# One line of 68 steps through a mixture's four blocks, and copies and splits of the causal heads on VectorE

## The reference

```
shared_out = silu(x @ shared_gate_w.T) * (x @ shared_up_w.T) @ shared_down_w.T
...
gate, up = jnp.split(gu, 2, axis=-1)
hmid = jax.nn.silu(gate) * up
y = jnp.einsum('tei,ehi->teh', hmid, down_proj)
out = jnp.einsum('teh,te->th', y, combine) + shared_out
```

```
score = jnp.einsum('bhqd,bhkd->bhqk', Q, K) / scale
score = score - 10000000000.0 * (1.0 - causal)
weights = jax.nn.softmax(score, axis=-1)
attn = jnp.einsum('bhqk,bhkd->bhqd', weights, V)
```

## Time and profile before

| | us |
|---|---|
| median of three runs | 1954.59 (1953.37 to 1954.68) |
| the profiled execution | 1949.53 |
| its span | 1947.7 |
| PE busy in the span | 1705.0 (88%) |
| VectorE busy | 1409.2 (72%) |
| ScalarE busy | 1158.7 (59%) |
| GpSimd busy | 311.4 (16%) |

### The profile page before, as it was taken

One profiled execution on the slowest core, in us unless ns is written; L12 is line 12 of the kernel. 1 busy time (PEld: TensorE's weight loads), 2 busy tenths in 40 slices (PEclk: granted clock), 3 DMA queues, 4 the chain that ended last, 5 costly groups with the idle time before them and its releaser, 6 DMA issues. The chain is left out here.

```text
span 1947.7 us, 44125 instructions
## 1 busy us (share of the span) xinstructions
PE 1705.0 (88%) x17561; PEld 804.5 (41%) x17561; DVE 1409.2 (72%) x2622; ACT 1158.7 (59%) x2294; POOL 311.4 (16%) x522
## 2 busy tenths in 40 slices
PE   3799999999999995889998798892599999999967
PEld 2222222222222223434444545881335555555546
DVE  5889999999999944765555407747788888888625
ACT  3278888888888893332222253551227777777744
POOL 0101000010000000000000346542003323111123
PEclk9789999999999997899997898996769999999988
DMA  4112111221111021043223279852401111111032
GB/s 141 35 43 70 62 51 50 76 66 59 50 51 38 24 49 68 1 88 92 90 82 142 76 233 338 259 167 84 157 24 36 34 29 34 32 32 32 7 90 81
DMA packets 78038, 154.52 MB, mean 79 GB/s; under 512 B 18685, under 2 KB 35965, under 8 KB 74137
## 3 DMA queue, kind: packets, MB, share of 16 engines
q1 hardware_dynamic: 63120, 121.47, 20.1%
q0 software_dynamic: 14384, 29.29, 4.7%
q10 hardware_dynamic: 328, 0.95, 0.1%
HBM read 102.23 MB, written 48.89 MB: 78 GB/s over the span
## 5 line engine op out<-in xcount | busy, mean ns | idle before, releaser
L848 ACT ACTIVATE heads_probs<-heads_pS 128x512 f32<-128x512 f32 (+3 forms) x1664 | 850.8, 573 | 170.1 <-PE heads_pS L714 154.5
L869 DVE TENSOR_REDUCE heads_run_max<-heads_pM 128x1 f32<-128x1024 f32 x512 | 592.8, 1217 | 54.8 <-PE heads_pM L736 53.4
L776 PE MATMUL heads_pO<-heads_probs,heads_vh 128*32 128x512 f32 (+2 forms) x3328 | 437.5, 570 | 1.4 <-ACT heads_probs L848 1.4
L714 PE MATMUL heads_pS<-heads_qs,heads_ks 75*32 75x512 bf16 (+3 forms) x4160 | 393.3, 370 | 6.9 <-ACT heads_probs L848 6.3
L880 DVE TENSOR_REDUCE heads_run_max<-heads_pM 128x1 f32<-128x512 f32 x384 | 246.9, 685 | 37.4 <-PE heads_pM L714 35.6
L714 PE MATMUL heads_pS<-heads_q_first,heads_ks 75*32 75x512 bf16 x2496 | 233.5, 377 | 10.5 <-ACT heads_probs L848 10.1
L714 PEld LDWEIGHTS heads_pS<-heads_qs,heads_ks 75*32 75x32 bf16 x4160 | 117.0, 95 | 176.6 <-issue 81.3
L714 PE MATMUL heads_pM<-heads_ks,heads_qs 72*32 72x512 bf16 (+3 forms) x1600 | 173.9, 359 | 1.2 <-DVE heads_run_max L880 0.5
L877 DVE CUSTOM_DVE_ANT_0 heads_masked_out<-heads_pM,heads_mask_end 128x128 bf16<-128x128 f32 (+3 forms) x256 | 121.9, 486 | 32.0 <-PE heads_pM L714 29.3
L776 PEld LDWEIGHTS heads_pO<-heads_probs,heads_vh 128*32 128x32 f32 x3328 | 107.9, 111 | 46.3 <-ACT heads_probs L848 2.8
L714 PEld LDWEIGHTS heads_pS<-heads_q_first,heads_ks 75*32 75x32 bf16 x2496 | 70.2, 95 | 128.0 <-ACT heads_probs L848 71.2
(11 more groups left out here) (383 smaller groups left out, 2401.9 us busy)
## 6 DMA issues: line engine op xcount, KB each, us to landing
top_weights<-k_comb_dram SPq DMA_DIRECT2D x128, 128.0 KB, 3.0
second_w<-in_L_W_dram SPq DMA_DIRECT2D x12, 1024.0 KB, 10.5
k_hid_slots_dram<-k_zeros SPq DMA_DIRECT2D x8, 1152.0 KB, 4.9
k_h_slots_dram<-second_work SPq DMA_DIRECT2D x48, 192.0 KB, 2.8
second_work<-k_hid_slots_dram SPq DMA_DIRECT2D x48, 192.0 KB, 3.8
k_parts_dram<-proj_part SPq DMA_DIRECT2D x12, 512.0 KB, 4.1
heads_ks<-k_parts_dram SPq DMA_DIRECT2D x63, 96.0 KB
heads_qs<-k_parts_dram SPq DMA_DIRECT2D x40, 96.0 KB
```

The lines of the kernel that those rows point to most:

```text
L714: mm = pe.matmul(out[cols, :], still[:, cols], moving, start=start, stop=stop)
L776: mm = pe.matmul(pO[k * 32:k * 32 + VW, int(second), o:BLK], vh[c][:, t, :], probs[u % 2][:, k * BLK + o:(k + 1) * BLK], start=first_chunk ...
L848: act.activation(probs[u % 2][:, k * BLK + c0 - b * BLK:(k + 1) * BLK], pS[:, slot, 0:c1 - c0], ACT.Exp)\
L869: dve.reduce_max(run_max[:, i, blocks[0][0] // 2:blocks[0][0] // 2 + 1], both.rearrange("p k c -> p (k c)"), AX.X).then_inc(taken, 2)
```

## The change

In `ffn_top6` the steps are numbered through all four blocks (m = 17 b + n), and the banks of `pG`, `pU`, `act_gate` and `hidden` alternate by m. `pY` gets two banks, by turns of the block. Step 16 of a block is closed after step 0 of the next has been opened; `yT` is copied behind the multiplications of step 0, the transposes stand on PE behind the close of step 1 (in the loop's turn n = 2), and the Silu of the result behind that of step 3. `add_residual` stays behind step 8.

In `attention_heads`, for the causal call alone, `split_max` runs on DVE directly behind `neg_max` and no more on POOL, and the two copies of a head's sums run on DVE, ahead of the last unit's pieces, and no more on ACT. Layer one keeps both as they were.

```diff
+        def split_max(queue, g):
+            queue.wait_ge(splitting, 4 * g + 1)
+            if g > 0:
+                queue.wait_ge(rows_in, 16 * PARTS * g)
+            queue.tensor_copy(max_parts[:, 0, :], neg_max[:, :]).then_inc(splitting, 1)
...
-                if exists(p, c + 1):
-                    split_max(h + 1)
+                if not causal and exists(p, c + 1):
+                    split_max(pool, h + 1)
...
             def keep_sums(h):
                 act.wait_ge(used, NU * (h + 1) + 2)
-                kept = act.activation(ot[h % ROUND][:, 0, :], pO[:, 0, :], ACT.Copy)
-                if causal:
-                    kept = act.activation(ot[h % ROUND][0:2 * 32, 1, :], pO[0:2 * 32, 1, :], ACT.Copy)
-                kept.then_inc(ot_kept, 1)
+                act.activation(ot[h % ROUND][:, 0, :], pO[:, 0, :], ACT.Copy).then_inc(ot_kept, 1)
...
-                    if n == RING and h > 0:
+                    if not causal and n == RING and h > 0:
                         keep_sums(h - 1)
...
-                dve.wait_ge(splitting, 4 * g + 1)
+                if causal:
+                    split_max(dve, g)
+                else:
+                    dve.wait_ge(splitting, 4 * g + 1)
...
                 for u in range(NU):
+                    if causal and u == NU - 1:
+                        dve.wait_ge(used, NU * (h + 1) + 2)
+                        dve.tensor_copy(ot[c][:, 0, :], pO[:, 0, :])
+                        dve.tensor_copy(ot[c][0:2 * 32, 1, :], pO[0:2 * 32, 1, :]).then_inc(ot_kept, 1)
...
-        pY, pR = S.ps("pY", [P, BLK]), S.ps("pR", [P, BLK])
+        pY, pR = S.ps("pY", [P, 2, BLK]), S.ps("pR", [P, BLK])
...
+        TURN_BEHIND = 2
...
             def close_step(b, n):
-                pe.wait_ge(mixed, STEPS * b + n + 1)
+                m = STEPS * b + n
+                if n == 0 and b >= 2:
+                    pe.wait_ge(y_kept, b - 1)
+                pe.wait_ge(mixed, m + 1)
                 w = K.down1[:, n, :] if n < L1_J else K.sdown1[:, :]
-                pe.matmul(pY[:, :], w, hidden[:, n % 2, :], start=(n == 0), stop=(n == L1_J)).then_inc(downed, 1)
+                pe.matmul(pY[:, b % 2, :], w, hidden[:, m % 2, :], start=(n == 0), stop=(n == L1_J)).then_inc(downed, 1)
...
                     if n >= 1:
                         close_step(b, n - 1)
-                close_step(b, STEPS - 1)
...
+                    elif b >= 1:
+                        close_step(b - 1, STEPS - 1)
+                    if b >= 1 and n == TURN_BEHIND:
+                        turn_result(b - 1)
+            close_step(NB - 1, STEPS - 1)
+            turn_result(NB - 1)
...
+                    if b >= 1 and n == TURN_BEHIND + 1:
+                        gate_result(b - 1)
...
+                    if b >= 1 and n == 0:
+                        keep_result(b - 1)
+                    if b >= 1 and n == STEPS // 2:
+                        add_residual(b - 1)
```

More of the change, by code:

```diff
@@ L704, in _ @@
             take_v(0, 0)
-            split_max(0)
+            if not causal:
+                split_max(pool, 0)
             every_head(one_head)
@@ L856, in _ @@
             every_head(one_head)
-            keep_sums(HEADS - 1)
+            if not causal:
+                keep_sums(HEADS - 1)
         @block.vector
@@ L1319, in open_step, with turn_result @@
                     (K.sgate1[:, :], K.sup1[:, :])
[L1320 to L1321 removed]
+                pe.matmul(pG[:, m % 2, :], gw, x, start=True, stop=True)
+                pe.matmul(pU[:, m % 2, :], uw, x, start=True, stop=True).then_inc(opened, 1)
             def close_step(b, n):
[L1324 removed]
+                m = STEPS * b + n
+                if n == 0 and b >= 2:
+                    pe.wait_ge(y_kept, b - 1)
+                pe.wait_ge(mixed, m + 1)
                 w = K.down1[:, n, :] if n < L1_J else K.sdown1[:, :]
[L1326 removed]
+                pe.matmul(pY[:, b % 2, :], w, hidden[:, m % 2, :], start=(n == 0), stop=(n == L1_J)).then_inc(downed, 1)
+            def turn_result(b):
+                if b >= 1:
+                    pe.wait_ge(g_kept, b)
+                pe.wait_ge(y_kept, b + 1)
+                for t in range(TPB):
+                    mm = pe.transpose(pR[:, t * P:(t + 1) * P], yT[:, t * P:(t + 1) * P], K.ident[:, :])
+                mm.then_inc(y_turned, 1)
             for b in range(NB):
@@ L1349, in _ @@
                    .then_inc(g_kept, 1)
+            for b in range(NB):
+                for n in range(STEPS):
+                    m = STEPS * b + n
+                    act.wait_ge(opened, m + 1)
+                    if m >= 2:
+                        act.wait_ge(mixed, m - 1)
+                    act.activation(act_gate[:, m % 2, :], pG[:, m % 2, :], ACT.Silu).then_inc(gated, 1)
+                    if b >= 1 and n == TURN_BEHIND + 1:
+                        gate_result(b - 1)
+            gate_result(NB - 1)
         @block.vector
@@ L1374, in body @@
+            for b in range(NB):
+                for n in range(STEPS):
+                    m = STEPS * b + n
+                    dve.wait_ge(gated, m + 1)
+                    if m >= 2:
+                        dve.wait_ge(downed, m - 1)
+                    mix = dve.tensor_tensor(hidden[:, m % 2, :], act_gate[:, m % 2, :], pU[:, m % 2, :], ALU.mult)
                     if n < L1_J:
                         mix.then_inc(mixing, 1)
-                        m = L1_J * b + n
-                        dve.wait_ge(mixing, m + 1)
@@ L1378, in body @@
-                        dve.wait_ge(weights_in[m % L1_RING], 32 * (m // L1_RING + 1))
-                        mix = dve.tensor_tensor(hidden[:, n % 2, :], hidden[:, n % 2, :], weights[:, m % L1_RING, :],
+                        k = L1_J * b + n
+                        dve.wait_ge(mixing, k + 1)
+                        dve.wait_ge(weights_in[k % L1_RING], 32 * (k // L1_RING + 1))
+                        mix = dve.tensor_tensor(hidden[:, m % 2, :], hidden[:, m % 2, :], weights[:, k % L1_RING, :],
@@ L1380, in body @@
                                                 ALU.mult)
                     mix.then_inc(mixed, 1)
-                    if n == STEPS // 2:
-                        for k in before:
-                            add_residual(k)
-                dve.wait_ge(downed, STEPS * (b + 1))
-                dve.tensor_copy(yT[:, :], pY[:, :]).then_inc(y_kept, 1)
-            body(0, [])
-            for b in range(1, NB):
-                body(b, [b - 1])
+                    if b >= 1 and n == 0:
+                        keep_result(b - 1)
```

45 lines of the change are left out of this document (15 added, 30 removed).

## The result

| | before | after |
|---|---|---|
| median of the runs, same chip | 1953.98 (4 runs) | 1939.22 (4 runs) |
| the profiled execution | 1949.53 | 1937.82 |
| its span | 1947.7 | 1936.0 |

The ratio is 0.9924, 95% interval 0.9911 to 0.9936: the kernel became 14.8 us faster. The forecast was 12.3 us and 1942.3. The two profiled executions differ by 11.7 us only, since before's lies 4.5 us under its median and after's 1.4 under.

The account below looks back on a forecast made before the run. PE was taken to set the pace in the feed-forward and causal heads. Feed-forward 7.3 us plus heads 5.0 (15 x (0.1 + 0.25) = 5.2, less 0.2 for the last copy) made 12.3, so 1942.3 us; range 1934 to 1950.

Parts of the forecast that it names:

- The feed-forward: Layer two's feed-forward: PE's 2.44 us of idle time goes at three of four block ends, 7.3 us, bounds 4 and 8.
- The rival in which the line does not close up: Feed-forward: the copy or a block's first multiplication still holds PE, half of 7.3 stays, 1945.9 us; chance 0.07.
- the 1.38 and the 1.4 us: Causal heads: if chained VectorE copies cannot overlap, the two take 1.38 us and the heads give 1.4 us less.
- The sums: Causal heads: copies of the sums moved from ScalarE to VectorE gain PE 0.25 us per head, bounds -0.2 and 0.48.
- the pair starts 0.26 earlier, at most: VectorE's pair behind a head's copies: cover 1.55 us less 1.29 for the copies leaves 0.26, limiting PE's gain.
- The sign that was named: At a head's start, PE's wait on ScalarE would be replaced by a shorter one on VectorE's copy.
- The split: Causal heads: splitting the row maxima on VectorE instead of POOL gains 0.1 us per head, bounds 0 and 0.26.
- the cover: VectorE's 0.92 us idle before the masked 128x512 reduction, to hide 0.84 us of split operations, leaving 0.08.
- the rival in which both waits are lost whole: Heads: VectorE is never late, PE loses waits of 0.26 and 0.48 us per head, 11.1 us; total 1936.2; chance 0.13.
- the two in which VectorE takes the gain back: Heads: VectorE gives back all they win, 1947.3 us, chance 0.2; or becomes their bound, 1966.8 us, chance 0.05.
- The 26.3 us: Length of a causal head before the change, computed as (1867.4 - 1472.8) / 15.
- a head of 26.0 us: Length of a causal head expected in the changed kernel's profile, as one sign of the forecast.

## Why the prediction was right, and where it was right by luck

**The feed-forward: right in each step.** Predicted 3 x 2.44 = 7.3, measured 195.5 less 188.2 = 7.3; with this part alone the stage has 188.2 too, and the ratio of the runs gives 6.9 (3.8 to 9.9). The closes run on at 2.575, no idle time is left, and the copy sits in VectorE's 1.16 and leaves 0.56 (forecast 0.4, since an operation follows the one before after 0.60 and not after its 0.69). The transposes cost 0.43 and not 0.49. The rival in which the line does not close up is out.

**The rule of the Trainium skill** (VectorE: DVE Perf Modes, "The DRAIN you can't avoid") was put aside for the row, and the runs agree with the row: three copies that follow each other are 0.60 apart for 0.69 of length. The prediction quoted the rule without its exception: the same section says that a next operation that is not held starts earlier. So the 1.38 and the 1.4 us that it worked out by the rule hold only for held operations, and these copies did start earlier.

**The sums: 0.34 a head where 0.25 was said.** The step that bounded it was "the pair starts 0.26 earlier, at most". It worked with 1.29 us for the copies. They took 1.20, and the 64x512 one is as dear as the other (0.67), as assumed. With the 0.09 that this leaves, 0.25 becomes 0.34, which is what the kernel with the sums alone measured. VectorE is what comes late next, as forecast: a third copy lengthens a quiet head by 0.56 to 0.60, and taking the second away gains 0.12. The sign that was named, a shorter wait on VectorE's copy in place of the one on ScalarE, is there.

**The split: 0.27 a quiet head where 0.1 was said; this step failed.** The prediction took the wait of PE for a bank to grow by what VectorE is late. The wait stayed 0.16. The four operations held the ones behind them by 0.75, not 0.84; the cover was 0.92 at that place, so by the same working 0.17 were to be had; the quiet heads gave all 0.26. (On the slower chip the heads with indirect writes gave nothing.) The masked operation of 512 now starts 2.04 us behind the maximum (1480.58 to 1482.62) and did so 2.29 behind it before (1490.06 to 1492.35). So it moved with PE by the same 0.25, where the working let it gain only 0.08: the 0.92 had been a wait for a product of PE, which itself came earlier once the turn in front of it did.

**The sum of the heads: right by luck.** 15 x 0.62 are 9.3 us, near the rival in which both waits are lost whole (11.1), and far from the two in which VectorE takes the gain back. What brought it back to 4.1 over the 15 periods, and 4.9 from copy to copy, is for the most part a term that the prediction does not have. It named what the split would do to VectorE and forgot what its going would do to GpSimd's list: a pair of indirect writes behind it was set free to run 2.7 us ahead of the loads of the maxima. The three periods in which PE waits for such a load, the fourth, seventh and fifth, cost 2.8 + 1.1 + 0.3 = 4.2 us of the 9.3, in one of them with a fallen clock. That the writes are their cause is shown by the kernels that hold the pair back, where the waits go, and by the one that moves the writes, where they move along; how the writes delay a load stays open. Of the other 1.0 us, 0.4 are the second period's, and 0.5 the first's, whose cause is open.

The head's own length was off too. The 26.3 us are the mean of 15 gaps between copies, of which the last two, beside the heads that run out, are short (25.67 and 22.21); from turn to turn an undisturbed head took 26.65. So "a head of 26.0 us" came out (26.03) by luck: the step to it was 0.62 and not 0.35.

**The total.** 12.3 forecast, 14.8 in the medians, 11.7 in the profiled executions. The reading of single executions can't decide between these: they moved by 2.1 ahead of the first edit and by 2.1 behind the last.

## What to carry to other kernels

When an operation is moved from one engine to another, read the list of the engine that loses it as closely as that of the one that gets it. What stood behind it is released earlier, and if it is a transfer it can land on one that somebody waits for. An idle time that is itself a wait for the engine you speed up moves with it, so cover of that kind can be larger than its row shows, as the 0.92 was here; test it by adding a copy of known length, since the point where it ends is where the next change of this kind begins to lose. And a sum that comes out right should be checked head by head: here two errors of some 4 us hid each other.

## What the runs showed of the hardware

- VectorE's price for a copy from the accumulation banks did not go with the number of partitions: 0.67 us for 64x512 beside 0.69 for 128x512; ScalarE had 0.58 and 0.60.
- A chain of 128x16 operations that wait for each other ran at 0.21 us from start to start on VectorE (0.17 busy), and at 0.28 on GpSimd (1790.19, 1790.47, 1790.75 and 1791.03 in the trace with the sums alone).
- A wait of PE of 1.41 us was followed by a granted clock of 0.79 and 0.64 in the next two stretches of 3 us, one of 1.13 (the last period of the kernel with late writes) by 0.70 and 0.73; one of 1.03 was followed by 1.00, and so was one of 0.85.
- The issue of three small loads on SyncE's queue took 4.98 us behind two indirect writes of GpSimd, and 1.82 or 1.83 in most heads; at the same place it took 2.43 in the kernel before, whose pair comes behind the split, and 2.79 with no writes near it.
- One and the same kernel took 1954 us on one chip and 2019 or 2020 on three others. In the heads the difference is bound to GpSimd's indirect writes: 28.5 us for a head with them against 26.65, at a granted clock of 1.00. In these heads PE pauses where the profile shows nothing that it waits for. The trace of the kernel with the feed-forward alone, weight loads of PE:

```profile
1576.36 0.13 PEld L714 LDWEIGHTS heads_pM<-heads_ks,heads_qs 72*32 72x32 bf16 x4 [0.57 <-issue]
...
1593.67 0.10 PEld L714 LDWEIGHTS heads_pS<-heads_q_first,heads_ks 75*32 75x32 bf16 x4 [0.57 <-issue]
```

  What holds PE there is open: no run here told the supply of instructions from anything else that the writes could disturb.
